# A transformer block and a quantised gated block: the softmax product in runs of four key tiles, q and k stacks in three places, V in two buffers on the chip

## The chip, the core and the metric

One core of a Trainium2 chip runs the whole program in one launch. The metric is the device time in microseconds of one execution; the kernel before took 1111.65 us (median of three runs, 1110.89 to 1113.03). All numbers of a trace come from one profiled execution. In it DVE is VectorE, ACT ScalarE, POOL GpSimd, SP SyncE (it only issues DMAs here), PE TensorE's matmuls and PEld its weight loads; SPq stands for SyncE's queue.

## The reference, cut to what matters

Eight sequences (batches) of 512 tokens with 256 features go through two layers. What the change touches is the attention of the first:

```python
def _ada_rmsnorm(x, t, gamma_w, beta_w):
    return (t @ gamma_w.T)[:, None, :] * _rmsnorm(x) + (t @ beta_w.T)[:, None, :]

def _attention(x, W_q, W_k, W_v, W_o):          # 16 heads of 16 features
    q, k, v = split(x @ W_q.T), split(x @ W_k.T), split(x @ W_v.T)
    attn = softmax(scale * einsum('bnqd,bnkd->bnqk', q, k), axis=-1)
    o = einsum('bnqk,bnkd->bnqd', attn, v)
    return o.transpose(0, 2, 1, 3).reshape(b, l, dm) @ W_o.T

x = x + a_alpha * _attention(_ada_rmsnorm(x, t, ...), W_q, W_k, W_v, W_o)
x = x + f_alpha * _swiglu(_ada_rmsnorm(x, t, ...), gate_w, hidden_w, out_w, out_b)
# then the second layer: rmsnorm, value * gelu(gate), 8-bit rows, ternary down_w, residual
```

## The kernel before

Each engine runs its own program, written out by hand, and they meet at semaphores (`need(engine, name, per, b, k)` waits until `name` has reached `b*per+k`). The attention layer is a software pipeline over the batches: iteration i has 32 slots z, and in each slot every engine does what the timetable (`T_...` constants) puts there for up to three batches, batch i+1 at times 0 to 31, batch i at 32 to 63, batch i-1 from 64. A slot z of the text is such a time modulo 32. The second layer starts in the last slots of iteration 7 and is not touched, but for where its buffers lie.

For a batch the order is: norm, transposed (T_XT1=3), q and k in four pieces (T_QK 7, 8, 10, 11), V in two (T_V 12, 13), then from T_MAX=18 one slot for every two row tiles of maxima, from T_ST=29 one slot m for every two score tiles, the softmax product, and at T_OT=65 the output's turn, its projection (T_OP, slots 4 and 5), the first residual `x1_` (VectorE, one slot later, lines 964 to 969), the second norm (slots 7 to 11), gate and hidden products in slots 14 to 28 and the down products two slots after each.

In TensorE's program a slot is, in this order: `shift_turn` in the four slots in which a group of four heads has all its maxima (times 26, 34, 42, 50, slots 26, 2, 10, 18; L1255), else the first `scores_max` (L1251); two `scores` matmuls (L1265); the weighted product where it is due; the `scores_max` that the turn put off, which waits for VectorE's first two operations on the turned maxima (`shift_c`, L931 and L933); the second `scores_max`; then `turn_o`, projections, q/k/v, gate and down products (L1162), and the turn of a finished group (`turn_group`, L1285). `scores_max` has two banks: matmul n waits for maximum n-2 (`maxima`, L924).

The maxima and scores read `qst` and `kst`, in which q and k of each head stand as six 16-row pieces of bf16 parts (and three rows of negated maxima in `qst`, from `shift`). Those come by way of DRAM: `store_parts` writes q and k parts, `stack` reads them back, 12 DMAs each time. V goes the same way: into `v3` (`v_high`, ScalarE), to `v_d`, and in two halves back to `vst` (`v_load`).

`exp` (ScalarE, L712) writes a pair of heads into one of six places of `p32`, two matmuls' worth per slot. `weighted(b, m)` is one key tile of a group: four heads side by side in the columns of the array, 32 columns each, two instructions each (eight in the trace). It is called twice in every fourth slot, so a block of L1277 has 16 instructions and two key tiles.

SyncE's program is in order, so every DMA waits behind the waits of those before. In an iteration it goes: x2 of two batches ago, al, V's second half, `shift(i, 1)`, `load_xr(i)` (waits until both halves of `x1_` of the batch before are done, L450), `load_xa(i+2)` (L444), parts 0 and 1 of the next batch, `shift(i, 2)`, `stack(nxt, 0)`, parts 2 and 3, `shift(i, 3)`, V's store and first half, `shift(nxt, 0)`, `stack(nxt, 1)`.

Of the kernel before, what the change touches and what calls it, by code (L numbers as in the profile page):

```python
# [16 lines left out]
F32 = mybir.dt.float32  # L17
# [7 lines left out]
P = 128  # L25
# [6 lines left out]
def build(nc, x, cond, w, out):  # L32
# [32 lines left out]
    T_PV = T_ST + 2  # L65
    T_OT = T_PV + STEPS + 2
# [8 lines left out]
    UP_ORDER = (0, 1, 4, 5, 2, 3, 6, 7)  # L75
# [4 lines left out]
    NP_BUF = 6  # L80
    NG = H // GROUP

# [14 lines left out]
    with ExitStack() as ctx:  # L97
# [11 lines left out]
        v_d = nc.dram_tensor("v_d", (B, P, TT, H, VW), F32).ap()  # L109
# [6 lines left out]
        wqkv = [sb(f"wqkv{i}", [P, KD, 3 * D], F32R) for i in range(2)]  # L116
# [33 lines left out]
        v3 = sb("v3", [P, TT, H, VW])  # L150
# [21 lines left out]
        vst_flat = vst[:, :, :, :].rearrange("p t h w -> p (t h w)")  # L172
        n_cw = len(KINDS) * KD * C
        cw = vst_flat[:, 0:n_cw].rearrange("p (n k c) -> p n k c", n=len(KINDS), k=KD)
        raw_o = vst_flat[:, n_cw:n_cw + KD * D].rearrange("p (n i) -> p n i", i=D)
# [6 lines left out]
        wup = [nc.alloc_sbuf_tensor_at(f"wup{n}", [P, KD, 2 * F], F32R, offset=stack_at + n * H * S * 2) for n in range(2)]  # L182
        raw_hp = nc.alloc_sbuf_tensor_at("raw_hp", [P, 2 * KD * S], F32, offset=hp_at)
        v3_flat = v3[:, :, :, :].rearrange("p t h w -> p (t h w)")
        vst_all = vst[:, :, :, :].rearrange("p t h w -> p (t h w)")
        raw_up = [v3_flat.rearrange("p (n i) -> p n i", i=D), raw_hp[:, :].rearrange("p (n i) -> p n i", i=D)]
# [6 lines left out]
        xn_b = tiles_p32[5].rearrange("p (t d) -> p t d", d=D)  # L193
        xr_b = vst_all[:, 0:TT * D].rearrange("p (t d) -> p t d", d=D)
        x1_b = vst_all[:, TT * D:2 * TT * D].rearrange("p (t d) -> p t d", d=D)
        h32_b = qk3[:, :, :, :].rearrange("p a n t -> p (a n t)")[:, 0:2 * KD * S].bitcast(F32).rearrange("p (k t) -> p k t", k=KD)
        qi = [v3_flat.bitcast(BF16)[:, F * n:F * (n + 1)] for n in range(2)]
        qT = [v3_flat.bitcast(BF16)[:, F * (2 + n):F * (3 + n)] for n in range(2)]
# [40 lines left out]
        qk_mm qk_h qk_r qk_m qk_l v_mm v_h parts0_st parts1_st v_st stack0_ld stack1_ld v0_ld v1_ld  # L239
# [8 lines left out]
        s = {n: sem(n) for n in names}  # L248

        def need(eng, name, per, b, k):  # L250
# [95 lines left out]
        def stack_part(eng, st, which, parts, b, tile, h0, h1, name):  # L346

            for g, part in enumerate(parts):
                stack_rows(eng, st, which, g, part, b, tile, h0, h1, name)

        def stack_rows(eng, st, which, g, part, b, tile, h0, h1, name):

            eng.dma_start(st[g * DH:(g + 1) * DH, tile * HT + h0:tile * HT + h1, :],
                          parts_d[bass.ds(b, 1), which, part, tile * P + h0 * DH:tile * P + h1 * DH, :].rearrange("o (h d) t -> d (o h) t", d=DH)).then_inc(s[name], 16)
# [5 lines left out]
        def first_rows(eng, st, which, parts, part):  # L360

            for g, p in enumerate(parts):
                if p == part:
                    stack_rows(eng, st, which, g, part, 0, 0, 0, GROUP, "stack_first")

        @block.sync
        def _(sp):
# [1164 lines left out]
```

## Time and profile before

| | before |
|---|---|
| median of three runs (us) | 1111.65 |
| profiled execution, its own time | 1110.89 |
| its span, first to last instruction | 1109.1 |
| mean granted TensorE clock | 0.980 |
| TensorE busy | 94% |
| VectorE busy | 70% |
| ScalarE busy | 51% |
| GpSimd busy | 31% |
| mean DMA rate | 84 GB/s |

The first attention batch starts its scores at 53 us; from 226 to 720 us six batches follow at 98.8 us each; the second layer alone runs from about 838 us to the end. The clock column of a windows row is the mean granted clock in it, 1.00 being 2.4 GHz and 0.50 1.2 GHz. A matmul's row includes its way through the array, so rows of successive matmuls overlap. "Idle before" is given with what ended it.

### The profile page before, as it was taken

What the parts mean: (1) busy time and instruction counts of PE and PEld (TensorE: products, weight loads), DVE (VectorE), ACT (ScalarE), POOL (GpSimd) and SP (SyncE); (2) the same over time, 40 slices, a digit from 0 to 9 for tenths busy, and PEclk for the clock granted to TensorE, in tenths of its full rate; (3) what the DMA queues carried; (4) which work ended last, traced back from release to release, by engine and by line L of the source; (5) the groups of instructions that cost most, each with busy time, mean ns of one, the idle gap of its engine ahead of it and who ended that gap; (6) DMA issues with size and microseconds to landing.
All of it is one profiled execution on the core that took longest, in us unless ns stands there. A gap on an engine that the chain in (4) does not pass through costs nothing.

```text
span 1109.1 us, 19198 instructions
## 1 busy us (share of the span) xinstructions
PE 1037.1 (94%) x6775; PEld 719.0 (65%) x6775; DVE 774.6 (70%) x1556; ACT 562.6 (51%) x1260; POOL 347.4 (31%) x415
## 2 busy tenths in 40 slices
PE   6789889999999999999999999988989999899997
PEld 5333247755774775577567567744878878788775
DVE  4766686677578757866876696677647787466775
ACT  4355666557556655755665575556552333132221
POOL 2501123323242332424133332201332444243331
PEclk9889999999999999999999999998999999999998
DMA  8554433064234406332531623060311210002111
GB/s 252 150 92 154 76 104 132 15 110 125 87 45 111 148 21 111 101 111 30 121 116 58 111 71 123 12 139 20 97 53 29 59 57 30 29 29 63 58 53 38
DMA packets 89375, 92.71 MB, mean 84 GB/s; under 512 B 11856, under 2 KB 86616, under 8 KB 88256
## 3 DMA queue, kind: packets, MB, share of 16 engines
q1 hardware_dynamic: 87248, 89.59, 31.1%
q10 hardware_dynamic: 2032, 1.90, 0.6%
q8 instruction: 54, 0.88, 0.3%
q14 instruction: 41, 0.34, 0.1%
HBM read 61.68 MB, written 29.78 MB: 82 GB/s over the span
## 4 chain that ended last, share of the span: by engine, by line
PE 77%; DVE 14%; issue 5%; DMA 2%; POOL 1%; ACT 1%; ACTq 0%; POOLq 0%; DVEq 0%
PE gen L1162 30%; PE core L1162 13%; PE pvb L1277 11%; PE core L1251 9%; PE core L1265 8%; DVE negmax L924 7%; PE gen L1488 2%; PE pvb L1480 1%; PE gen L1236 1%; DVE o L948 1%; PE pvb L1285 1%; PE gen L1315 1%; PE core L1255 1%; DVE qs L1112 1%; DMA shift_d<-shift 0%
## 5 line engine op out<-in xcount | busy, mean ns | idle before, releaser
L924 DVE TENSOR_REDUCE negmax<-core 128x1 f32<-128x512 f32 x512 | 337.5, 684 | 169.9 <-PE core L1251 169.0
L712 ACT ACTIVATE p<-core 128x512 f32<-128x512 f32 x512 | 278.5, 597 | 146.1 <-PE core L1265 143.5
L1162 PE MATMUL gen<-hs,wgh 128*128 128x256 f32 x1536 | 220.5, 294 | 9.7 <-DVE a L978 9.7
L1251 PE MATMUL core<-kst,qst 96*128 96x512 bf16 x512 | 193.7, 395 | 33.5 <-DVE negmax L924 27.7
L1162 PEld LDWEIGHTS gen<-hs,wgh 128*128 128x128 f32 x1536 | 196.2, 189 | 28.3 <-DVE a L978 14.8
L1162 PE MATMUL core<-wup,hp 128*128 128x512 f32 x768 | 190.7, 397 | 0.9 <-POOL hp L652 0.9
L603 POOL TENSOR_TENSOR a<-a 128x256 fp32r<-128x256 f32 x128 | 94.7, 740 | 290.3 <-ACT a L730 287.7
L1162 PEld LDWEIGHTS core<-wup,hp 128*128 128x128 f32 x768 | 140.2, 189 | 29.2 <-issue 0.9
L1265 PE MATMUL core<-qst,kst 99*128 99x512 bf16 x512 | 157.2, 387 | 0.1
L1251 PEld LDWEIGHTS core<-kst,qst 96*128 96x128 bf16 x512 | 46.0, 97 | 152.3 <-DVE negmax L924 77.4
L1277 PE MATMUL pvb<-p,vst 128*32 128x512 f32 x1024 | 127.7, 618 | 0.0
L730 ACT CAST a<-a 128x256 fp32r<-128x256 f32 x128 | 52.0, 406 | 126.8 <-DVE a L978 84.4
L1162 PE MATMUL gen<-wout,a 128*128 128x256 f32 x768 | 113.8, 286 | 2.4 <-DVE h L918 1.7
L1162 PEld LDWEIGHTS gen<-wout,a 128*128 128x128 f32 x768 | 100.7, 190 | 4.6 <-DVE h L918 1.9
L1106 DVE TENSOR_TENSOR p<-core,p 128x512 f32<-128x512 f32 x64 | 44.1, 688 | 71.2 <-PE core L1162 50.3
L660 POOL TENSOR_SCALAR v<-p 128x1024 bf16<-128x1024 f32 x32 | 34.5, 1078 | 149.7 <-DVE p L1120 149.7
L725 ACT ACTIVATE th<-gen 128x256 f32<-128x256 f32 x128 | 48.7, 381 | 50.8 <-PE gen L1162 50.1
L1265 PEld LDWEIGHTS core<-qst,kst 99*128 99x128 bf16 x512 | 50.7, 100 | 33.4 <-ACT p L712 6.7
L1277 PEld LDWEIGHTS pvb<-p,vst 128*32 128x32 f32 x1024 | 27.2, 111 | 67.5 <-issue 64.9
L862 ACT ACTIVATE p<-core 128x512 f32<-128x512 f32 x64 | 37.8, 590 | 62.7 <-PE core L1162 62.6
L974 DVE SCALAR_TENSOR_TENSOR ug<-th,gen 128x256 f32<-128x256 f32 x128 | 52.7, 411 | 19.0 <-ACT th L725 18.8
L574 POOL TENSOR_TENSOR hp<-h,hp 128x512 fp32r<-128x512 f32 x15 | 21.5, 1454 | 116.0 <-ACT hp L705 116.0
(158 smaller groups left out, 1234.0 us busy)
## 6 DMA issues: line engine op xcount, KB each, us to landing
parts_d<-qk SPq DMA_DIRECT2D x30, 384.0 KB, 2.7
v_d<-v SPq DMA_DIRECT2D x8, 1024.0 KB, 3.9
vst<-v_d SPq DMA_DIRECT2D x16, 512.0 KB, 5.4
qst<-parts_d SPq DMA_DIRECT2D x96, 64.0 KB, 2.3
qst<-parts_d SPq DMA_DIRECT2D x48, 128.0 KB, 4.5
kst<-parts_d SPq DMA_DIRECT2D x48, 128.0 KB, 7.7
kst<-parts_d SPq DMA_DIRECT2D x91, 64.0 KB, 2.3
xr<-in_x_dram SPq DMA_DIRECT2D x8, 512.0 KB, 4.0
```

Of the source, the lines that this page charges most:

```text
L603: pool.tensor_tensor(a2[1][:, n % 2, :], a32[:, n % 2, :], a2[0][:, n % 2, :].bitcast(F32), ALU.subtract).then_inc(s["a_lo"], 1)
L712: act.activation(p32[:, ring(b, m), k * S:(k + 1) * S], stb[k], ACT.Exp, scale=SCALE).then_inc(s["exp_"], 1)
L725: act.activation(th[:, n % 2, :], gh_bank(b, n)[:, 0:HALF], ACT.Tanh, scale=0.5).then_inc(s["tanh_"], 1)
L730: act.copy(a2[0][:, n % 2, :], a32[:, n % 2, :]).then_inc(s["ah"], 1)
L862: act.activation(ge[:, c, :], smb[c], ACT.Gelu).then_inc(s["gelu"], 1)
L924: dve.tensor_reduce(negmax[:, n // TT, n % TT:n % TT + 1], smb[n % 2], AX_X, ALU.max, negate=True).then_inc(s["smax"], 1)
L974: dve.scalar_tensor_tensor(out=ug[:, n % 2, :], in0=th[:, n % 2, :], scalar=1.0, in1=gh_bank(b, n)[:, 0:HALF], op0=ALU.add, op1=ALU.mult). ...
L1106: dve.tensor_tensor(hb[t % 2][:, c * S:(c + 1) * S], stb[c], ge[:, c, :], ALU.mult).then_inc(s["hmul"], 1)
L1162: last = pe.matmul(out_, l, r, start=start and i == 0, stop=stop and i == len(passes) - 1, **kw)
L1251: pe.matmul(smb[n % 2], qst[0:KROWS, h, q * P:(q + 1) * P], kst[0:KROWS, h, :], start=True, stop=True).then_inc(s["smax_mm"], 1)
L1265: last = pe.matmul(stb[k], kst[0:KROWS + NPART, h, kt * P:(kt + 1) * P], qst[0:KROWS + NPART, h, :], start=True, stop=True)
L1277: last = pe.matmul(pvb[j * VW:(j + 1) * VW, :], vst[:, kt, GROUP * g + j, :], p32[:, ring(b, m - 1 + j // 2), (j % 2) * S:(j % 2 + 1) * S] ...
```

## The change

The two `weighted` calls of every fourth slot become four in every eighth: the product of a group's four key tiles is one run, in times T_PV+7, +15, +23 and +31 with T_PV=30, slots 5, 13, 21, 29. It stands at the end of the softmax part of the slot, after both `scores_max`. `p32` gets eight places. `turn_group`, `o_out` and `heads_out` follow T_PV and come one slot earlier; T_OT and all after it stay. For the room, `qst` and `kst` hold 12 heads instead of 16, in three places of four heads that the groups take in turn (`place`), and each group is loaded by itself: group 3 in its own iteration after `load_xa`, group 0 where tile 0 was, group 1 after `shift(i, 3)`, group 2 where tile 1 was. Each load waits until the group that had the place has all its scores (`place_free`). V no longer goes to DRAM: `v_high` writes into `v0` or `v1` by the batch's parity and the product reads there. In the second layer `wup`, `xn_b` and others lie elsewhere, and the order of eight weight groups differs.

```diff
-    T_PV = T_ST + 2
-    T_OT = T_PV + STEPS + 2
+    T_PV = T_ST + 1
+    T_OT = T_PV + STEPS + 3
...
-    NP_BUF = 6
+    NP_BUF = 2 * KT
     NG = H // GROUP
+    N_PLACES = 3
...
-        qst = sb("qst", [P, H, S], BF16)
-        kst = sb("kst", [P, H, S], BF16)
-        vst = sb("vst", [P, TT, H, VW])
+        qst = sb("qst", [P, N_PLACES * GROUP, S], BF16)
+        kst = sb("kst", [P, N_PLACES * GROUP, S], BF16)
+        v1 = sb("v1", [P, TT, H, VW])
+        vbuf = (v0, v1)
...
+        def place(b, g):
+            return (b * NG + g + 1) % N_PLACES * GROUP
...
-            def stack(b, tile):
+            def place_free(b, g):
+                if g >= N_PLACES:
+                    need_sp("st_mm", 2 * STEPS, b, 4 * GROUP * (g + 1 - N_PLACES))
+                else:
+                    need_sp("st_mm", 2 * STEPS, b - 1, 4 * GROUP * (NG + g + 1 - N_PLACES))
+            def stack(b, g):
                 for n in range(2):
-                    need_sp(f"parts{n}_st", 16 * KD, b, 16 * (tile + 1))
-                pieces = ((0, GROUP, "stack_first"), (GROUP, HT, "stack0_ld")) if tile == 0 else ((0, HT, "stack1_ld"),)
-                for h0, h1, name in pieces:
-                    need_sp("st_mm", 2 * STEPS, b - 1, 4 * (tile * HT + h1))
-                    for st, which, parts in ((qst, 0, Q_PARTS), (kst, 1, K_PARTS)):
-                        stack_part(sp, st, which, parts, b, tile, h0, h1, name)
+                    need_sp(f"parts{n}_st", 16 * KD, b, 16 * (g * GROUP // HT + 1))
+                place_free(b, g)
+                for st, which, parts in ((qst, 0, Q_PARTS), (kst, 1, K_PARTS)):
+                    stack_part(sp, st, which, parts, b, g, STACK[g])
...
                 if here:
-                    v_load(i, 1)
                     shift(i, 1)
                     load_xr(i)
                 if i + 2 < B:
                     load_xa(i + 2)
+                if here:
+                    stack(i, 3)
...
                 if prep:
-                    need_sp("v_h", TT // 2, nxt, TT // 2)
-                    sp.dma_start(v_d[bass.ds(nxt, 1), :, :, :, :].rearrange("o p t h w -> p (o t h w)"), v3[:, :, :, :]).then_inc(s["v_st"], 16)
-                    if i == -1:
-                        sp.wait_ge(s["cw2_t"], 1)
-                        sp.wait_ge(s["wt_t"], 1)
-                    v_load(nxt, 0)
+                    if i != -1:
+                        stack(nxt, 1)
                     shift(nxt, 0)
                 if i == -1:
-                    stack(0, 1)
+                    stack(0, 2)
...
                 if here and prep:
-                    stack(nxt, 1)
+                    stack(nxt, 2)
...
+                    if i == -1 and z == Z_REST + 2:
+                        pool.wait_ge(s["cw2_t"], 1)
+                        pool.wait_ge(s["wt_t"], 1)
+                        pool.memset(v1[:, :, :, DH:VW], 1.0).then_inc(s["v1_ones"], 1)
...
             def v_high(b, j):
                 need(act, "v_mm", TT // 2, b, j + 1)
-                need(act, "v_st", 16, b, 0)
-                act.copy(v3[:, 2 * j:2 * j + 2, :, 0:DH], gen[V_BANK[j]][:, :].rearrange("p (t h d) -> p t h d", t=2, h=H)).then_inc(s["v_h"], 1)
+                need(act, "pv_mm", NG * KT, b - 1, 0)
+                if (b, j) == (1, 0):
+                    act.wait_ge(s["v1_ones"], 1)
+                act.copy(vbuf[b % 2][:, 2 * j:2 * j + 2, :, 0:DH], gen[V_BANK[j]][:, :].rearrange("p (t h d) -> p t h d", t=2, h=H)).then_inc(s["v_h"], 1)
...
             def weighted(b, m):
                 g, kt = m // (2 * KT), m % (2 * KT) // 2
-                if kt == 0 and g % 2 == 0:
-                    need(pe, f"v{g // 2}_ld", 16, b, 16)
+                if kt == 0 and g == 0:
+                    need(pe, "v_h", TT // 2, b, TT // 2)
...
-                    for b, m in stream(z, T_PV):
-                        if m % 4 == 3:
-                            weighted(b, m - 2)
-                            weighted(b, m)
                     for b, g in turned:
                         need(pe, "shift_c", 4 * NG, b, 4 * g + 2)
                         for b2, m in stream(z, T_MAX):
                             scores_max(b2, 2 * m)
                     for b, m in stream(z, T_MAX):
                         scores_max(b, 2 * m + 1)
+                    for b, m in stream(z, T_PV):
+                        if m % (2 * KT) == 2 * KT - 1:
+                            for kt in range(KT):
+                                weighted(b, m - 2 * (KT - 1 - kt))
```

## Rows read from the trace of the kernel before

**Rows 1.** the page's chain that ended last; the windows view of one steady period
```profile
PE 77%; DVE 14%; issue 5%; DMA 2%; POOL 1%; ACT 1%; ACTq 0%; POOLq 0%; DVEq 0%
...
325.47:424.23 98.76, 95.25 (x663) 64.55 (x662) 71.32 (x140) 60.53 (x134) 32.68 (x36) 1.00 0.36 91
```

**Rows 2.** timeline of TensorE, batch 4: start, length, line, count, idle before and releaser
```profile
424.22 0.39 PE L1251 MATMUL core<-kst,qst 96*128 96x512 bf16 x1
...
426.05 0.60 PE L1265 MATMUL core<-qst,kst 99*128 99x512 bf16 x2
426.57 1.92 PE L1277 MATMUL pvb<-p,vst 128*32 128x512 f32 x16
428.43 0.39 PE L1251 MATMUL core<-kst,qst 96*128 96x512 bf16 x1
...
433.02 0.39 PE L1251 MATMUL core<-kst,qst 96*128 96x512 bf16 x1 [1.25 <-DVE negmax L924]
...
440.90 0.39 PE L1251 MATMUL core<-kst,qst 96*128 96x512 bf16 x1
...
458.47 0.60 PE L1251 MATMUL core<-kst,qst 96*128 96x512 bf16 x2
...
462.58 0.39 PE L1251 MATMUL core<-kst,qst 96*128 96x512 bf16 x1
```

**Rows 3.** timeline of VectorE in the same batch
```profile
431.66 0.25 DVE L944 RECIPROCAL orec<-pvb 128x16 f32<-128x16 f32 x1
...
432.28 2.51 DVE L924 TENSOR_REDUCE negmax<-core 128x1 f32<-128x512 f32 x4
...
438.97 1.28 DVE L958 TENSOR_TENSOR hs<-gen,hs 128x512 fp32r<-128x512 f32 x2
...
449.81 0.69 DVE L969 TENSOR_TENSOR x<-ug,xr 128x512 f32<-128x512 f32 x1
```

**Rows 4.** timeline of TensorE's weight loads inside one block
```profile
427.03 0.13 PEld L1277 LDWEIGHTS pvb<-p,vst 128*32 128x32 f32 x4 [0.30 <-issue]
427.46 0.13 PEld L1277 LDWEIGHTS pvb<-p,vst 128*32 128x32 f32 x4 [0.30 <-issue]
```

**Rows 5.** timelines of TensorE and VectorE at the turn of slot 26
```profile
413.13 0.27 PE L1255 MATMUL core<-ident,negmax 128*16 128x128 f32 x1
413.24 0.60 PE L1265 MATMUL core<-qst,kst 99*128 99x512 bf16 x2
...
413.75 0.28 DVE L933 TENSOR_TENSOR shift<-core,shift 16x128 f32<-16x128 f32 x1
```

**Rows 6.** SyncE: timeline of its issues; waits of SyncE, of TensorE (total, times, longest)
```profile
450.53 0.40 SPq L450 DMA_DIRECT2D xr<-in_x_dram  x1
451.02 0.45 SPq L444 DMA_DIRECT2D xa<-in_x_dram  x1
...
472.34 2.77 SPq L353 DMA_DIRECT2D kst<-parts_d  x6
...
SPq L450 <- DVE x L969: 66.6, 7, 10.2
...
PE core L1251 <- DMA kst<-parts_d: 0.8, 1, 0.8
```

**Rows 7.** line 353 between 462 and 475: time from issue to landing
```profile
DMA to landing us min/median/max: 2.1/2.3/3.5
```

**Rows 8.** windows view: last columns clock, share of the DMA engines, GB/s
```profile
426.10:428.10 2.00, 2.00 (x19) 0.47 (x17) 1.22 (x3) 1.40 (x3) 0.73 (x1) 1.00 1.15 140
452.50:456.30 3.80, 3.51 (x20) 2.03 (x19) 3.80 (x9) 3.80 (x9) 1.07 (x2) 1.00 0.79 256
470.50:472.50 2.00, 2.00 (x16) 1.57 (x15) 1.05 (x3) 0.82 (x3) 0.00 (x0) 1.00 0.48 136
```

**Rows 9.** windows view: a thin stretch of batch 0 and what followed it
```profile
98.80:102.60 3.80, 2.30 (x11) 0.68 (x9) 3.40 (x8) 2.17 (x4) 0.00 (x0) 1.00 0.51 139
102.70:106.00 3.30, 3.30 (x17) 0.59 (x16) 0.79 (x4) 1.04 (x2) 0.00 (x0) 0.50 0.72 246
```

More of the change, by code:

```diff
@@ L343, in rows_of, with stack_part, stack_rows @@
             return t[bass.ds(b, 1), :, :].rearrange("o (t p) d -> p (o t) d", p=P)
[L346 to L354, printed above, removed]
+        def stack_part(eng, st, which, parts, b, g, name):
+            for n, part in enumerate(parts):
+                stack_rows(eng, st, which, n, part, b, g, name)
+        def stack_rows(eng, st, which, n, part, b, g, name):
+            h0, r0 = place(b, g), g * GROUP * DH
+            eng.dma_start(st[n * DH:(n + 1) * DH, h0:h0 + GROUP, :],
+                          parts_d[bass.ds(b, 1), which, part, r0:r0 + GROUP * DH, :].rearrange("o (h d) t -> d (o h) t", d=DH)).then_inc(s[name], 16)
         def first_part(eng, which, part, name):
@@ L363, in first_rows @@
                 if p == part:
-                    stack_rows(eng, st, which, g, part, 0, 0, 0, GROUP, "stack_first")
+                    stack_rows(eng, st, which, g, part, 0, 0, "stack_first")
         @block.sync
@@ L413, in first_stack @@
                 first_rows(sp, kst, 1, K_PARTS, 2)
[L414 removed]
+                stack_part(sp, qst, 0, Q_PARTS, 0, 1, "stack1_ld")
                 for name in ("first_kh", "first_km"):
                     sp.wait_ge(s[name], 16)
[L417 to L424 removed]
+                stack_part(sp, kst, 1, K_PARTS, 0, 1, "stack1_ld")
             def shift(b, g):
@@ L431, in shift @@
                 need_sp("shift_st", 16 * (H // GROUP), b, 16 * (g + 1))
-                need_sp("st_mm", 2 * STEPS, b - 1, 4 * GROUP * (g + 1))
-                sp.dma_start(qst[KROWS:KROWS + NPART, g * GROUP:(g + 1) * GROUP, :],
+                place_free(b, g)
+                sp.dma_start(qst[KROWS:KROWS + NPART, place(b, g):place(b, g) + GROUP, :],
                              shift_d[bass.ds(b, 1), :, n0:n1, :].rearrange("o n (h j) t -> (o n) h (j t)", h=GROUP)).then_inc(s["shift_ld"], 16)
@@ L558, in _ @@
             pool.memset(half_pow[:, :], -0.5).then_inc(s["consts_set"], 1)
[L559 removed]
+            pool.memset(v0[:, :, :, DH:VW], 1.0).then_inc(s["consts_set"], 1)
             pool.wait_ge(s["consts_set"], 3)
@@ L844, in first_half @@
                     if b == 0 and t == 0:
-                        last = max(m for m in range(STEPS) if ring(B - 1, m) == NP_BUF - 1)
-                        act.wait_ge(s["pv_mm"], NG * KT * (B - 1) + (last | 3) // 2 + 1)
+                        act.wait_ge(s["st_mm"], 2 * STEPS * B)
                     need(act, f"x2_ld{t}", 16, b, 16)
@@ L1242, in scores_max @@
             def scores_max(b, n):
-                for first, name in ((0, "stack_first"), (TT * GROUP, "stack0_ld"), (TT * HT, "stack1_ld")):
+                for first, name in ((TT * GROUP * g, STACK[g]) for g in range(NG)):
                     if n == first:
@@ L1262, in scores @@
                 for k in range(2):
-                    h = GROUP * g + 2 * pair + k
+                    h = place(b, g) + 2 * pair + k
                     need(pe, "exp_", 2 * STEPS, b, 2 * m + k - 1)
@@ L1276, in weighted @@
                 for j in range(GROUP):
-                    last = pe.matmul(pvb[j * VW:(j + 1) * VW, :], vst[:, kt, GROUP * g + j, :],
+                    last = pe.matmul(pvb[j * VW:(j + 1) * VW, :], vbuf[b % 2][:, kt, GROUP * g + j, :],
                                      p32[:, ring(b, m - 1 + j // 2), (j % 2) * S:(j % 2 + 1) * S], start=(kt == 0), stop=(kt == KT - 1))
```

50 lines of the change are left out of this document (22 added, 28 removed).

## The prediction, made before the changed kernel was run

> **What bounds the kernel now.** I read the page's engine shares and clock first (the table above), then the chain, then one period of the pipeline. The chain that ended last is 77% TensorE and 14% VectorE [rows 1]. One batch sequence takes 98.76 us in the steady part, TensorE busy 95.25 us of it [rows 1]. That figure hides something: one matmul's row is 0.39 us long, yet two in a row are 0.60 [rows 2], so each takes 0.22 us of TensorE and the rest of its row is its way through. I therefore count starts, not busy time. In that measure a slot (two matmuls of L1251 for the maxima, two of L1265 for the scores) takes 0.88 us, the softmax product (L1277) comes in every fourth slot, and in slots 14 to 29 gate and down products fill TensorE completely. In slots 31 to 9 VectorE is the slower engine: before 433.02 TensorE waits 1.25 us for a maximum [rows 2], while VectorE makes four maxima in 2.51 us without a pause [rows 3]. So the kernel alternates between a stretch bound by TensorE and a stretch in which the two take turns, and what an edit is worth depends on which it lands in.
>
> **The merged products.** Before, a block is four groups of four matmuls (two key tiles, two passes each). The weight loads of successive groups start 0.43 us apart (427.03, 427.46) [rows 4]. Four groups are 1.72 us, but the scores end at 426.05+0.22+0.22=426.49, the block starts at 426.57 and the next matmul at 428.43 [rows 2]: it takes 1.94 to 1.95 us. So entering and leaving cost 0.23 us per block. The change makes 32 blocks of eight groups (3.44+0.23=3.67 us) out of 64: it saves 32×0.23=7.4 us, 0.92 per batch. This lies on TensorE and counts in full.
>
> **What the old places covered.** Blocks stood in slots 2, 6, 10, 14, 18, 22, 26, 30; now they stand in 5, 13, 21, 29. The turns of the maxima (L1255) are in slots 2, 10, 18, 26, each of which had a block, and none has one now. After a turn at 413.13 the scores end at 413.24+0.44=413.68; VectorE's second shift operation ends at 413.75+0.28=414.03, and only then may the next L1251 go [rows 5]. The block, which stood there, hid that wait. Without it TensorE waits about 0.40 us. Slots 18 and 26 are in the full stretch: 0.80 us per batch on the path, against 0.46 saved by their two merges.
>
> Slots 29 to 3, with times from the first L1251 of slot 29 (424.22). After: slot 29 is 0.88+3.67+0.72=5.3; slot 30 with down and the group's turn 2.0, to 7.3. Then VectorE sets the pace, at 0.60 a maximum, 0.62 for the heads' output, 0.60 for the scaling, 1.2 for the four shift operations, 1.2 for both residues of o (each the distance between two starts: 432.28-431.66, and (2.51-0.69)/3 or 1.28-0.68 for rows of several [rows 3]): from 7.45 the heads' output, slot 31's maxima and the scaling to 9.9, slot 0's to 11.1, slot 1's until 12.3; the turn starts at 12.4, the shift operations end at 13.9, maxima and residues at 16.35. The next slot's L1251 needs the last maximum before that plus a residue's time: slot 4 starts at 17.1. Before it was 440.90-424.22=16.7 [rows 2]. The blocks that left slots 30 and 2 were partly cover for VectorE, and the time they gave back is gone: +0.4.
>
> **The stack of group 3.** Before, all sixteen heads had their own place, and q and k of the last eight were loaded in the batch sequence before. With three places group 3 must wait for group 0's scores (slot 4), and in SyncE's program it stands behind load_xr, which waits for the first residual (x1_), and behind load_xa. L450 follows the VectorE row of L969 that ends at 450.50, and L444 comes 0.49 us later [rows 3, 6]; SyncE waits 66.6 us for that residual in all [rows 6]. The residual after: slot 4 takes 2.25 (17.1 to 19.4), slot 5 with block and projection 0.88+3.67+1.42, to 25.3; two maxima and two operations of 0.6 and 0.7 end it at 28.4. Then 1.0 us for the issues of xr and xa, eleven spacings of 0.47 between twelve pieces (six take 2.77 us [rows 6]), and 2.3 us for the last to land [rows 7]: at best 28.4+1.0+5.2+2.3=36.9. xr and xa are in front, though; most of their 1 MB moves from 452.5 to 456.3, 5.8 us after the residual, at 256 GB/s [rows 8]. Behind them 0.77 MB of pieces at that rate take 3.0 us and 0.4 for the completion: 37.6. At the 140 GB/s which larger pieces showed between 426 and 428 [rows 8] it would be 28.4+5.8+5.5=39.7. I take 37.6, since the small pieces moved 136 GB/s at a share of only 0.48, the large ones 140 at 1.15 [rows 8]. The Trainium skill ("DMA: Bandwidth & Descriptors", "Anatomy of one DMA") gives, for transfers that GpSimd issues, a fixed 2.0 us plus the bytes at 436 GB/s, 2.15 us for 64 KB. By that estimate the best case would be 36.75 rather than 36.9; the row's 2.3 us is used.
>
> When does TensorE want it? Slot 6 runs 25.3 to 26.6. VectorE ends the residual at 28.4, and then owes the heads' output and slot 7's maxima: slot 8 begins at 29.7, slot 9 at 31.95, the turn of slot 10 at 33.9, its first L1251 at 35.0, which is the first to read group 3. (Before: 458.47-424.22=34.25, with three blocks in it [rows 2].) So the load is late by 2.6 us, bounds 1.9 and 4.7. Behind the waiting L1251 stand the q and k projections of slots 10 and 11. From that L1251 to slot 12 are 462.58-458.47=4.1 us [rows 2]: slot 12 starts at 41.7, before at 38.4. That is +3.3, and with 0.35 for slots 12 to 28 **+3.7 us per batch** (bounds 3.0 and 5.8).
>
> **Everything else.** ACT's first exponential of a group now waits for the first key tile of the block, some 1.4 us; tanh, h_high and the casts queue behind it. The closest is h_high in slot 5, then GpSimd's remainders (2×1.3 us), wanted in slot 7 1.3 us later than I find them done: nothing, or 1 us per batch if that margin is wrong. V: eight stores and sixteen loads go from SyncE's queue; no TensorE or VectorE wait names them, only SyncE's own [rows 6], so nothing gained. The copy of V now waits for the product two batches back, long done. The memset of the second V's ones runs while GpSimd is idle; behind it stand small operations of the next preparation, no price, at most its own microsecond or so. The other stack loads (groups 0, 1, 2 in slots 13, 21, 29) have five slots each of 2 to 6 us against 5.5 us of issue and 2.3 of landing: covered; if slot 29's were late by its whole landing it would cost 2.3 per batch. The tail's new buffers and order touch no row on its path.
>
> **Sum.** Batches 1 to 5: 5×3.7=18.5. Batch 6 has no xa in front (0.5 less): 3.2. Batch 7 has no xa either and no maxima after slot 17, so its late turns cost nothing while the merges save 0.46: 3.3-0.5-0.46=2.3. Batch 0 has no residual to wait for, and no gates: of eight slots two had a block, 0.88+1.95 and that with the turn's 0.11, 5.8 together. Now one has 0.88+3.67 and one the turn, its wait and two maxima, about 1.7: 6.25, or +0.45, four times 1.8. Together 25.8 us, the 7.4 saved already taken off.
>
> **The clock.** Between 98.8 and 102.6 TensorE started only 11 matmuls, and from 102.7 to 106.0 the granted clock was 0.50 (1.2 instead of 2.4 GHz) [rows 9]. In the steady period it stayed 1.00 [rows 1], though slots 31 to 1 are thin there too. After the change slots 31 to 3 are thin for 10 us, and the wait in slot 10 is idle time. A fall costs half of its 3.3 us, about 1.6, if full work follows. I count one fall in every second of seven batches: +5 us (bounds 0 and 11, one in each). By the Trainium skill ("TensorE: Matmul & The Clock Gate", "Why this matters for your kernels") an idle gap between bursts of matmuls puts TensorE back to half rate. That speaks against this change; by it every batch would have its fall, and the sum would be 6 us higher.
>
> The profiled execution took 1110.89 us around a span of 1109.1; the median of three is 0.76 above it. So 1110.89+25.8+5+0.8=1142.5, and I say **1142**.
>
> **Rivals.** (1) *No stack wait*: the load is in time, because the residual comes earlier or the pieces overlap. Then the turns and VectorE's stretches remain: in slots 29 to 9 about +1 net of merges, slots 12 to 28 +0.35, so 1.4 a batch, 10 in all: 1121 (1116 to 1128). For it: a single wait of TensorE for a stack, 0.8 us, is in the trace now [rows 6]. Against it: that stack is loaded with nothing but its slot in the way. (2) *The merges win*: the waits after turns and in slots 31 to 9 are absorbed, since VectorE gets to work ahead during a block. Price 7.4 saved: 1104. It decides if the uncovered wait is under 0.23×32/28=0.26 us; the row says 0.40, and two banks for the maxima let VectorE get only two ahead. (3) *It costs more*: pieces at 140 GB/s (+2.1 a batch) and a clock fall in every batch: 1142+15=1157, up to 1162. (4) *It doesn't do what it says*: the eight groups are torn apart by a late exponential. Its last one is issued a slot before, so no; it would give back the 7.4: 1149.
>
> **Chances.** Forecast (1128 to 1148) 0.48, (3) and (4) 0.18, (1) 0.20, (2) 0.10, no change 0.04. A measurement of this kernel tells 0.2%, some 2.2 us, from nothing. Range: 1118 to 1158, which leaves out (2), no change and the far ends of (1) and (3). Faster 0.10, same 0.04, slower 0.86.
>
> **What would show it.** Blocks of L1277 of 32 rows lasting about 3.65 us; a wait of 0.4 us before L1251 after each L1255; a wait of L1251 for the DMA of kst or qst once per batch of 2 to 3 us, in slot 10; a period of about 102.5 to 103; clock 0.96 to 0.98. Wrong, if that DMA wait is missing (rival 1), or if slots 31 to 3 are shorter than 1.7 us each.

## The result: 3.8% slower, and where the time went

The changed kernel takes **1153.27 us** (median of four runs, 1150.21 to 1156.36) against 1111.27 for the kernel before (four runs, 1108.71 to 1113.03). The ratio is 1.038, 95% interval 1.0349 to 1.0412. The direction was forecast and the time lies in the range of 1118 to 1158, but 11 us above the 1142. The profiled execution of the changed kernel took 1156.36 us around a span of 1154.6.

| | before | after |
|---|---|---|
| median (us) | 1111.27 | 1153.27 |
| span of the profiled execution | 1109.1 | 1154.6 |
| mean granted TensorE clock | 0.980 | 0.959 |
| TensorE / VectorE busy | 94% / 70% | 91% / 67% |
| mean DMA rate | 84 GB/s | 66 GB/s |

The timeline of TensorE shows where each batch's scores start. By those starts (span against span, 45.5 us in all) the loss is distributed so: batch 0 takes 67.7 us instead of 73.9 (-6.2); batch 1 106.4 instead of 99.35 (+7.0); batches 2 to 6 105.2 to 106.1 instead of 98.8 to 99.1 (together +34.3); batch 7 100.35 instead of 94.42 (+5.9); from its last scores to the second layer's first unit 14.2 instead of 11.87 (+2.3); the rest +2.1. Batches 2 to 6 are the steady part, five batches and not six from 226 to 720 us before.

The page of the changed kernel: the clock by slices, then the chain that ended last. VectorE has gone from 14 to 16% of the chain and the engine "issue" from 5 to 6% [rows 1].

```profile
PEclk9799889998999999999989999987998999999998
...
PE 74%; DVE 16%; issue 6%; POOL 1%; DMA 1%; ACT 1%; ACTq 0%; POOLq 0%; DVEq 0%
```

One steady period of it in the windows view (width, busy and count of TensorE, its weight loads, VectorE, ScalarE, GpSimd; clock, share of the DMA engines, GB/s):

```profile
439.06:544.29 105.23, 96.95 (x663) 65.62 (x661) 70.55 (x140) 60.60 (x134) 32.27 (x36) 0.98 0.23 66
```

It has the same 663 rows of matmuls as a period before [rows 1], so nothing was added to TensorE's work. The 6.5 us more went to idle time and to a lower clock. The waits of TensorE (total, times, longest) say at what:

```profile
PE core L1259 <- DVE negmax L932: 29.0, 53, 2.0
PE core L1259 <- issue: 25.1, 7, 4.7
...
PE core L1259 <- DVE shift L941: 6.6, 24, 0.7
```

The second line is the load of group 3. The view names "issue" since it saw no releaser, but it comes seven times, once in each of batches 1 to 7 and always in slot 10. The third is the uncovered turn: 24 waits, where before there was one of 0.7 us. Batch 4 on TensorE's timeline (start, length, ..., idle time before it and its releaser):

```profile
439.06 0.39 PE L1259 MATMUL core<-kst,qst 96*128 96x512 bf16 x1
...
440.02 3.64 PE L1285 MATMUL pvb<-p,v 128*32 128x512 f32 x32
...
452.61 0.60 PE L1259 MATMUL core<-kst,qst 96*128 96x512 bf16 x2 [0.25 <-DVE shift L941]
...
456.18 0.39 PE L1259 MATMUL core<-kst,qst 96*128 96x512 bf16 x1
...
473.14 0.28 PE L1263 MATMUL core<-ident,negmax 128*16 128x128 f32 x1
473.25 0.60 PE L1273 MATMUL core<-qst,kst 99*128 99x512 bf16 x2
477.60 0.59 PE L1259 MATMUL core<-kst,qst 96*128 96x512 bf16 x2 [3.75 <-issue]
477.84 2.22 PE L1170 MATMUL gen<-hp,wqkv 128*128 128x512 f32 x6
```

The block is whole, 32 rows in 3.64 us (so are 30 of the kernel's 32 blocks). After the scores at 473.25 TensorE stands for 3.75 us. The six projection matmuls behind the wait take 2.22 us; with the wait short (the next experiment) they take 1.73. What SyncE issued meanwhile (same batch), and how long those twelve pieces took to land:

```profile
467.66 0.39 SPq L455 DMA_DIRECT2D xr<-in_x_dram  x1
468.15 0.45 SPq L449 DMA_DIRECT2D xa<-in_x_dram  x1
468.72 2.78 SPq L361 DMA_DIRECT2D qst<-parts_d  x6
471.54 2.77 SPq L361 DMA_DIRECT2D kst<-parts_d  x6
...
DMA to landing us min/median/max: 3.6/4.5/5.3
```

The last piece is issued near 473.9 and TensorE goes on at 477.60. Before, the same kind of piece landed in 2.3 us [rows 7]. The windows view shows why (last columns: clock, share, GB/s), and last, what the clock did behind the wait:

```profile
469.60:471.60 2.00, 2.00 (x10) 1.33 (x10) 2.00 (x5) 2.00 (x5) 1.10 (x2) 1.00 0.99 328
471.60:473.60 2.00, 1.97 (x14) 1.24 (x12) 2.00 (x6) 2.00 (x5) 0.00 (x0) 1.00 1.15 282
473.60:475.60 2.00, 0.25 (x2) 0.00 (x0) 1.60 (x5) 1.66 (x4) 1.41 (x2) 1.00 1.15 200
475.60:477.60 2.00, 0.01 (x1) 0.04 (x2) 0.00 (x0) 0.00 (x0) 0.89 (x1) 1.00 1.07 271
...
478.90:482.30 3.40, 3.40 (x9) 1.77 (x9) 2.90 (x5) 1.91 (x4) 0.00 (x0) 0.50 0.01 5
```

The DMA engines are full from 469.6 until the stack has landed, and in this batch, 1.3 us after TensorE starts again, the granted clock is 0.50 (1.2 GHz) for 3.4 us. Such a stretch, called a fall below, begins in or just behind the wait of slot 10 in each of batches 1 to 6 (from 158.0, 263.8, 369.7, 478.9, 581.3 and 687.1; five of them are 6.8 us long), and none in the steady period before [rows 1].

### The profile page after: what moved, and what is told of

The parts are those of the page before. It is cut to its first block, busy times and chain, and to the rows that moved or that the text cites. A ratio compares the mean times of both kernels' runs of the same rounds, so it can differ in the third digit from the quotient of the medians.

```text
span 1154.6 us, 19269 instructions
## 1 busy us (share of the span) xinstructions
PE 1055.1 (91%) x6775; PEld 731.1 (63%) x6775; DVE 771.0 (67%) x1556; ACT 562.8 (49%) x1260; POOL 343.8 (30%) x416
## 4 chain that ended last, share of the span: by engine, by line
PE 74%; DVE 16%; issue 6%; POOL 1%; DMA 1%; ACT 1%; ACTq 0%; POOLq 0%; DVEq 0%
PE gen L1170 30%; PE core L1170 12%; PE pvb L1285 10%; PE core L1259 8%; DVE negmax L932 7%; PE core L1273 7%; PE gen L1498 2%; PE pvb L1490 1%; PE gen L1244 1%; PE pvb L1293 1%; DVE shift L941 1%; DVE shift L939 1%; DVE shift L943 1%; DVE o L956 1%; DMA parts_d<-qk 1%
## 5 line engine op out<-in xcount | busy, mean ns | idle before, releaser
L1259 PE MATMUL core<-kst,qst 96*128 96x512 bf16 x512 | 202.4, 409 | 62.2 <-DVE negmax L932 29.0
L1273 PE MATMUL core<-qst,kst 99*128 99x512 bf16 x512 | 163.1, 398 | 0.3 <-ACT p L719 0.2
L1259 PEld LDWEIGHTS core<-kst,qst 96*128 96x128 bf16 x512 | 47.9, 99 | 156.6 <-DVE negmax L932 74.8
L1285 PE MATMUL pvb<-p,v 128*32 128x512 f32 x1024 | 118.8, 605 | 0.0
L1285 PEld LDWEIGHTS pvb<-p,v 128*32 128x32 f32 x1024 | 30.3, 111 | 73.6 <-issue 73.2
L1170 PE MATMUL gen<-hp,wqkv 128*128 128x512 f32 x192 | 64.0, 475 | 0.0
```

What stands on the lines that cost most here:

```text
L1170: last = pe.matmul(out_, l, r, start=start and i == 0, stop=stop and i == len(passes) - 1, **kw)
L1259: pe.matmul(smb[n % 2], qst[0:KROWS, h, q * P:(q + 1) * P], kst[0:KROWS, h, :], start=True, stop=True).then_inc(s["smax_mm"], 1)
L1273: last = pe.matmul(stb[k], kst[0:KROWS + NPART, h, kt * P:(kt + 1) * P], qst[0:KROWS + NPART, h, :], start=True, stop=True)
L1285: last = pe.matmul(pvb[j * VW:(j + 1) * VW, :], vbuf[b % 2][:, kt, GROUP * g + j, :], p32[:, ring(b, m - 1 + j // 2), (j % 2) * S:(j % 2 + ...
```

## Experiments

All are edits of the changed kernel unless said otherwise. Ratios are against the kernel before, timed on the same chip. "The reordered kernel" is the first of them. Each has one profiled execution, and the number of falls differs between the executions of one kernel, so falls are counted in the profiled one.

**The stack of group 3 loaded ahead of xr and xa.** Its place is free after slot 4, so it need not stand behind load_xr, which waits for the residual.

```diff
                     shift(i, 1)
+                    stack(i, 3)
                     load_xr(i)
                 if i + 2 < B:
                     load_xa(i + 2)
-                if here:
-                    stack(i, 3)
```

> The changed kernel with one edit: group 3's stack is issued before load_xr and load_xa, so that it waits for group 0's scores alone. Theory A (the load behind the residual is the main loss): the idle of 3.75 us before the first L1259 of slot 10 goes, 3.5 us in each of 7 batches, and the clock falls that follow it (1.6 to 2.5 us each) go too; what is left over the kernel before is the uncovered turns and VectorE's stretch, 1.4 us a batch less nothing: 1118 to 1122 us, period 100.1 us. Rival B (the clock falls come from the thin slots 31 to 3, not from the idle wait): the wait goes and the falls stay, one or two per batch: 1128 to 1135 us. Rival C (the stack is late for another reason, such as the rate of its transfers): above 1145 us.

Measured: 1121.29 us (1120.43 to 1125.13), ratio 1.0113 (1.0085 to 1.0142). SyncE issues group 3's pieces from 440.78 now, and nothing is left of the wait in slot 10 but the turn's (batch 4, TensorE's timeline):

```profile
456.83 0.28 PE L1262 MATMUL core<-ident,negmax 128*16 128x128 f32 x1
456.94 0.60 PE L1272 MATMUL core<-qst,kst 99*128 99x512 bf16 x2
457.93 0.60 PE L1258 MATMUL core<-kst,qst 96*128 96x512 bf16 x2 [0.39 <-DVE shift L940]
458.18 1.73 PE L1169 MATMUL gen<-hp,wqkv 128*128 128x512 f32 x6
```

No fall of the clock is left in batches 1 to 6, though slots 31 to 3 are as thin as in the changed kernel. So **the order of one SyncE program cost 32 of the 42 us**, and the falls behind slot 10 came with the wait, not from the thin slots. The settled period is 100.7 to 100.8 us: 1.95 above the kernel before.

**Runs of two key tiles at the old places**, with the loads and V of the changed kernel.

```diff
-    T_PV = T_ST + 1
-    T_OT = T_PV + STEPS + 3
+    T_PV = T_ST + 2
+    T_OT = T_PV + STEPS + 2
...
-                    for b, m in stream(z, T_PV):
-                        if m % (2 * KT) == 2 * KT - 1:
-                            for kt in range(KT):
-                                weighted(b, m - 2 * (KT - 1 - kt))
...
                         scores(b, m)
+                    for b, m in stream(z, T_PV):
+                        if m % 4 == 3:
+                            weighted(b, m - 2)
+                            weighted(b, m)
```

> The changed kernel with the product put back into runs of two key tiles in slots 2, 6, 10 and so on; places, loads and V stay as changed. Theory A: group 3 is still late. The residual ends 26.3 us after slot 29 as before, the load needs 10.0 us from there as in the changed kernel, 36.3, and TensorE wants it at 34.25: 2 us a batch, 14 in all, 1125 us, up to 1135 where the clock falls behind it. Rival D (the loss belongs to the merged runs and their places alone): 1111 us, the kernel before.

Measured: 1123.29 us, ratio 1.0121 (1.0092 to 1.015). Counted from the residual the load takes as long as in the changed kernel (from the issue of xr to the L1259 of slot 10 10.6 us in batch 4, against 9.9; its pieces land in 4.8 us), but the wait is smaller:

```profile
PE core L1259 <- issue: 11.4, 6, 2.6
```

Here the block of 1.92 us stands in slot 10, between the turn and the L1259 that reads the late stack, while in the changed kernel that work stands in slot 5, ahead of the residual on which the load waits. So the blocks that moved away had hidden not only VectorE's shift but would have hidden half of this wait too (12.1 us over seven batches instead of 22.5), and with a shorter idle time only one fall of the clock was seen in batches 1 to 6.

**Both.** The two edits together; what is left of the change is V on the chip, the three places and eight buffers.

> Both edits: runs of two key tiles, and group 3's stack before load_xr. Against the kernel before only the three places, the ring of eight and V on the chip remain. Theory A: these cost nothing once the load is early: 1109 to 1113 us. Rival: keeping V on the chip or the ring of eight has a gain or a price of its own: outside that.

Measured: 1106.23 us (ten runs, 1101.46 to 1111.22; before 1110.55), **ratio 0.9961 (0.9939 to 0.9984)**: faster than both kernels, by a little, and below the 1109 to 1113 that were expected. The steady period is 98.87 to 98.90, that of before. Taking either edit alone leaves 1.1 to 1.2%, both together nothing, neither 3.8%: the parts are not a sum, since the removed cover and the late load meet in slot 10. Alone they cost 10.7 and 12.7 us, together 42. Of the 18.6 us more, 10.4 are the longer waits, and the rest is about what six falls cost instead of one.

**Sixteen heads again**, so that group 3 has a place of its own and is loaded a batch ahead as before. To make room, heads_out's raw output shares the last place of p32 and the second layer's down weights lie in the fourth place of kst.

```diff
-    N_PLACES = 3
+    N_PLACES = 4
...
-                if here:
-                    stack(i, 3)
...
                     stack(nxt, 2)
+                    stack(nxt, 3)
```

> Merged runs of four key tiles and V on the chip, but q and k stacks of all sixteen heads as before, group 3 loaded at the end of an iteration behind group 2 (the room comes from laying the copy of the product and the ternary weights over other buffers). Theory A: the merge alone costs more than it gives, 1.4 us a batch: 1118 to 1122 us, like the first experiment. Rival E (runs of four are a gain, the stacks spoil it): 7 us under the kernel before, 1104 us.

Measured: 1122.28 us, ratio 1.0123 (1.0095 to 1.0151). It agrees with the reordered load within its interval, and no fall is left in batches 1 to 6 either, so it is the late load that cost the 32 us and nothing else about the reordering. Runs of four key tiles are no gain even with every load in time.

**The wait filled with matmuls.** Fifteen matmuls of data that lie ready, whose result nobody reads, are added between the scores of slot 10 and the waiting L1259.

```diff
                     for b, g in turned:
+                        if g == 2 and 1 <= i < B:
+                            need(pe, "o_norm", NG, i, 1)
+                            for _ in range(15):
+                                pe.matmul(pvb[:, :], wo[0][:, 0, 0:P], wo[1][:, :, :].rearrange("p k n -> p (k n)"), start=True, stop=True)
```

> The changed kernel with fifteen matmuls more per batch (of weights, into the idle product bank, 0.236 us each, 3.5 us) between the scores of slot 10 and the maxima that wait for group 3. The load is as late as before. Theory A: TensorE's idle time in slot 10 is what makes the clock fall; with it filled the falls of 1.6 to 2.5 us in each of seven batches go and nothing is added, since the wait was there anyway: 1136 to 1143 us. Rival B (thin slots 31 to 3 make it fall): the falls stay, 1153 us. Rival F (work in the wait isn't free): above 1153 us.

Measured: 1142.36 us (1140.0 to 1147.05), ratio 1.0305 (1.0264 to 1.0347), clock 0.983. A kernel that does more work is 11 us faster. Batch 4 of it:

```profile
466.91 0.60 PE L1273 MATMUL core<-qst,kst 99*128 99x512 bf16 x2
467.16 3.81 PE L1414 MATMUL pvb<-wo 128*128 128x512 f32 x15
471.42 0.59 PE L1259 MATMUL core<-kst,qst 96*128 96x512 bf16 x2 [0.45 <-issue]
471.66 1.75 PE L1170 MATMUL gen<-hp,wqkv 128*128 128x512 f32 x6
```

From the turn's scores to the stack's arrival the same time goes by (4.5 us here, 4.35 in the changed kernel). What changes is the work after it: six projections in 1.75 instead of 2.22 us, and slots 10 to 12 (first L1259 to first L1259) 4.1 instead of 5.7. All six falls of slot 10 are gone: the stretch is 4.06 to 4.11 us in each of batches 1 to 6, where the changed kernel has 5.7 to 7.0. So they are caused by the idle wait and not by the late load as such.

The one fall left in these batches lies elsewhere, in slots 3 and 4 of batch 3, behind a thin stretch (windows view):

```profile
339.50:342.90 3.40, 2.22 (x10) 0.57 (x8) 3.24 (x8) 2.92 (x6) 0.00 (x0) 1.00 0.77 236
342.90:346.30 3.40, 3.40 (x13) 2.40 (x13) 2.10 (x4) 0.98 (x3) 0.00 (x0) 0.50 0.01 4
```

So thin slots can make the clock fall too (rival B), but rarely: once in these six batches, and not in batches 1 to 6 of the reordered kernel, of sixteen heads and of the two kernels below whose turns are covered.

**xa behind the stack.** Only load_xr stands ahead of it.

```diff
+                if here:
+                    stack(i, 3)
                 if i + 2 < B:
                     load_xa(i + 2)
-                if here:
-                    stack(i, 3)
```

> The changed kernel with load_xa issued after group 3's stack instead of before it; load_xr and the residual it waits for are still in front. In batches 1 to 5 the 512 KB of xa leave the way. If the stack is late by the bytes in front of it (the DMA engines' share is 1.0 to 1.15 all that time): 1.9 us less at 270 GB/s, 1143 us (1141 to 1146). If it is late by the issues on SyncE's queue alone: 0.5 us less, 1151 us.

Measured: 1139.06 us (1132.34 to 1144.73), ratio 1.0259 (1.0213 to 1.0305). The pieces' time from issue to landing, in the same batch:

```profile
DMA to landing us min/median/max: 2.4/3.3/4.1
```

So with both loads in front they take 4.5 us, with one 3.3, with none 2.3 (median in the reordered kernel, and [rows 7]). The bytes in front are a price of their own beside their issue: in batches 1 to 5 the L1259 of slot 10 comes 0.8 to 1.8 us earlier, and xa's issue is only 0.5 of it. The saving is larger than expected, since the shorter wait also left three falls in batches 1 to 6, of 3.4 us each, instead of six: behind waits of 3.3, 2.6 and 2.4 us, and none behind 2.1, 2.8 and 2.1.

**The turns covered.** The reordered kernel, and in the two slots of the full stretch that have a turn (18 and 26) the twelve gate and hidden matmuls go ahead of the pair that waits for VectorE's shift.

```diff
+                    gates = [(b, n) for n, t in enumerate(T_GH) for b in at(z, t)]
+                    if turned:
+                        for b, n in gates:
+                            gate_hidden(b, n)
+                        gates = []
                     for b, g in turned:
...
-                    for n, t in enumerate(T_GH):
-                        for b in at(z, t):
-                            gate_hidden(b, n)
+                    for b, n in gates:
+                        gate_hidden(b, n)
```

> The first experiment (1121.3 us) with the twelve gate and hidden matmuls of slots 18 and 26 moved ahead of the maxima that wait for the turned shift. By the prediction's step, an uncovered turn costs 0.40 us; twelve of them lie in the full stretch, so 4.8 us go: 1116.5 us (1115 to 1118), and the waits of L1259 for L941 become a third. Rival: VectorE gets its maxima later and the next slot waits for it instead: 1121 us or more.

Measured: 1129.8 us (1127.36 to 1131.83), ratio 1.0177 (1.0143 to 1.0212). That is **worse** than without, 1121.29, where 1116.5 was expected. Batch 4:

```profile
520.43 0.27 PE L1262 MATMUL core<-ident,negmax 128*16 128x128 f32 x1
520.54 0.60 PE L1272 MATMUL core<-qst,kst 99*128 99x512 bf16 x2
520.79 1.76 PE L1169 MATMUL gen<-hs,wgh 128*128 128x256 f32 x12
522.39 0.61 PE L1258 MATMUL core<-kst,qst 96*128 96x512 bf16 x2
...
524.95 0.39 PE L1258 MATMUL core<-kst,qst 96*128 96x512 bf16 x1 [0.56 <-DVE negmax L931]
...
530.03 0.95 PE L1169 MATMUL gen<-wout,a 128*128 128x256 f32 x6 [0.26 <-POOL a L604]
```

The wait for the shift is gone, and the slot takes 3.25 us (start of its scores to that of the next) instead of 3.61. But the pair of maxima starts 1.85 us after the scores instead of 0.85, behind the gates, VectorE reduces it later, and the next slot's second maximum waits for its bank at 524.95: slot 27 takes 3.75 instead of 3.01. Slot 28 takes 3.50 instead of 3.01, and there the row at 530.03 shows a wait for GpSimd. 0.4 us saved, 1.2 given back. The rival in the expectation (VectorE late) was right for the larger part of that.

**Half a cover.** The reordered kernel again. Of the twelve only the six gate matmuls go ahead; they take 0.9 us, enough for the shift.

```diff
+                    early = [(b, n) for n, t in enumerate(T_GH) for b in at(z, t)] if turned else []
+                    for b, n in early:
+                        need(pe, "a_", NCH, b, n if b == B - 1 else n - 1)
+                        gate_half(b, n, 0)
                     for b, g in turned:
...
-                            gate_hidden(b, n)
+                            if early:
+                                gate_half(b, n, 1).then_inc(s["gh_mm"], 1)
+                            else:
+                                gate_hidden(b, n)
```

> The first experiment (1121.3 us) with only the six gate matmuls (0.71 us) of slots 18 and 26 ahead of the maxima that wait for the turned shift; the six hidden ones stay behind. The shift is ready 0.36 to 0.40 us after the scores, so 0.71 us cover it, and the maxima start 0.3 us later than in the first experiment instead of 1.0. If the price of a turn is 0.40 us and what spoiled the full move was VectorE's late start (0.74 us more in each next slot), then up to 12 times 0.40 go: 1117 us (1115.5 to 1119). If VectorE is late at once, each turn gives back 0.3 or more: 1121 to 1125 us.

Measured: 1125.36 us (six runs, 1120.23 to 1127.86; before on that chip 1113.45), ratio 1.0094 (1.0066 to 1.0122). That is above the 1117 hoped for, but the interval overlaps that of the reordered kernel, so the time decides nothing. The trace is clearer: slots 18 and 26 take 3.22 instead of 3.65 and 3.61, the slots behind them (19 and 27) 0.07 more each, but slot 28 still takes 3.50, where a down product waits for GpSimd:

```profile
529.19 0.95 PE L1169 MATMUL gen<-wout,a 128*128 128x256 f32 x6 [0.26 <-POOL a L604]
```

That gives 0.2 us per batch of the 0.8. Why GpSimd's `a` comes late there when only the gates of slot 26 moved was not followed further.

**V alone on the kernel before**: two buffers on the chip, no stores and loads of V, all else as it was.

```diff
-            def v_load(b, tile):
...
+                act.copy(vbuf[b % 2][:, 2 * j:2 * j + 2, :, 0:DH], gen[V_BANK[j]][:, :].rearrange("p (t h d) -> p t h d", t=2, h=H)).then_inc(s["v_h"], 1)
```

> The kernel before with V kept in two buffers on the chip, nothing else. Theory: V's transfers were on no path; what made the third experiment 4 us faster than the kernel before is that the stack wanted in slot 2 of batch 1 is loaded in smaller pieces, earlier (a wait of 1.74 us and a clock fall there): 1109 to 1112 us. Rival G: V's transfers delayed that stack through SyncE's queue and the DMA engines, so V alone gives it: 1105 to 1107 us.

Measured: 1110.69 us (twelve runs), ratio 0.9995 (0.9974 to 1.0015). V costs and gains nothing, as the prediction had it. So the 0.4% of the best version doesn't come from V alone.

## Why the prediction came out as it did

All times of this section are from the first L1259 of slot 29 of batch 4, 439.06 in the changed kernel.

**Merges.** 3.64 us for 32 rows where 3.67 was forecast, 30 of 32 blocks whole. Right; rival (4) is out.

**Turns.** The working put 0.40 us on each uncovered turn. In the reordered kernel slots 18 and 26 show the idle time of 0.25 us before L1258 and take 0.36 to 0.43 us less once the wait is covered (3.22 to 3.25 instead of 3.65 and 3.61). Right. The idle time alone would not have decided against rival (2), whose limit was 0.26 us; the length of the slots does, and so do the 1121 and 1122 us of the two kernels with every load in time, where it said 1104. That the 0.4 us can be had back was not claimed, and they mostly can't.

**Slots 29 to 3.** Slot 4 begins at 456.18, 17.12 against 17.1. Right.

**The residual.** It decides when the load starts:

```profile
466.94 0.69 DVE L977 TENSOR_TENSOR x<-ug,xr 128x512 f32<-128x512 f32 x1
```

It ends at 28.57, forecast 28.4. The turn of slot 10 stands at 34.08, forecast 33.9. Right.

**The landing** is the first term that was mis-sized. Forecast 37.6 with bounds 36.9 and 39.7; the L1259 goes at 477.60, 38.54, and in batches 2 to 6 at 37.4 to 39.0. The choice of 37.6 took the 256 GB/s of xr and xa and let the pieces follow at that rate, with 0.4 us for completion, a term that no run shows by itself. That left 3.0 us from the last issue (34.6) to the end. The last piece was issued near 473.9 (34.8), where the forecast had it, but TensorE went on only 3.7 us later, though the rate was 200 to 328 GB/s: the engines were at a share of 1.0 to 1.15 to the end, and with fewer bytes in front the pieces land sooner. Over batches 1 to 7 the gap between the last L1259 of slot 9 and the first of slot 10 is 4.6 to 6.7 us, against 2.4 (3.0 in batch 7) in the reordered kernel: 22.5 us of wait in all, where 2.6 times seven is 18.

**Slots 10 to 12** were taken as the 4.1 us of before [rows 2]. In the changed kernel they take 5.7, and 6.3 to 7.0 in the other batches with a fall. All of that is the clock: where no fall follows the late load (the filled wait, and batches 4 to 6 with xa behind) they take 4.1. The reordered kernel, at a clock of 1.00, needs 0.45 us more than before there: its slot 11 takes 2.73 us instead of 2.27, both from scores to scores, and its projections wait 0.19 us there for VectorE's `h` (L917), which is behind. In the changed kernel the 4.1 at full clock says that VectorE has caught up during the wait. With slots 12 to 29, +0.6 instead of 0.35, and +0.9 instead of 0.75 in slots 29 to 9, the reordered kernel's period is 1.95 us over that of before, where the working without the late load implied 1.1 and rival (1) put 1.4.

**The clock** is the term that was furthest off. The mechanism was right: half rate after an idle wait. The count was wrong: one fall in every second batch was forecast, and in the profiled execution each of batches 1 to 6 has one. The price was too low as well: 1.6 us is what the one fall of 3.4 us costs, in batch 4, but five are 6.8 us long and cost 2.2 to 2.9 each. Slots 10 to 12 of batches 1 to 6 together take 13.9 us more than those of the filled wait; forecast were 5, with an upper bound of 11. Between the changed and the reordered kernel, 34.3 us apart by their spans, lie 22.5 of waits and 13.9 of clock, less the 2.7 (six times 0.45) that VectorE catches up, 33.7 in all. The profiled execution was the slowest of four; two of the others had a mean clock of 0.967 instead of 0.959, so they lost less to it. The rule of the Trainium skill that the prediction weighed ("TensorE: Matmul & The Clock Gate", "Why this matters for your kernels"), that an idle gap between bursts of matmuls puts TensorE back to half rate, held in batches 1 to 6 of the changed kernel, and the filled wait agrees with it; among the shorter waits, of up to 2.8 us, of the other kernels some were followed by a fall and some not.

**The signs** that the prediction named: blocks of 3.65 us (3.64), a wait for the shift after each turn (24 of 32; in seven of the others the load comes later), a wait in slot 10 of 2 to 3 us (2.4 to 4.7), a period of 102.5 to 103 (105.2 to 106.1), a clock of 0.96 to 0.98 (0.959). In batches 2 to 6 the period grew by 6.9 us where 3.7 and 0.7 for the clock were forecast: the landing is 0.8 of the difference, the clock 1.6.

**Batch 0** was forecast at +1.8 and is 6.2 shorter. Batch 0 ends, by this count, where batch 1's scores start. The block of group 3 now falls into batch 1 as a whole, where before half of it did: 1.9 us less, which come back in the tail. And batch 0 had three clock falls of 3.4 us before, at 71.9, 102.6 and 119.7; the changed kernel has one, of 6.8 from 117.1, and a clock of 1.00 where the first two were:

```profile
71.90:75.30 3.40, 3.40 (x18) 2.12 (x17) 3.12 (x6) 2.40 (x6) 1.36 (x2) 1.00 0.76 144
```

It isn't shown that the merge did this. The kernel before with V alone changed keeps runs of two, has none of the three falls in its profiled execution, and its batch 0 takes 68.5 us. So the falls of batch 0 come and go, and most of the gain here may be luck.

Batch 1 of the kernel before also held a wait for a stack that the prediction did not look at, and which is gone (it stays with V alone, 2.2 us, and is gone in every other kernel of this document, all of which load each group by itself):

```profile
140.69 0.59 PE L1251 MATMUL core<-kst,qst 96*128 96x512 bf16 x2 [1.74 <-issue]
```

Taken together, batches 0 and 1 of the reordered kernel are 7.3 us shorter than before's.

**Batch 7 and the tail.** Batch 7 was forecast at +2.3, and of the tail's new buffers and order it was said that they "touch no row on its path". Batch 7 is +5.9: its L1259 of slot 10 is 2.2 us later behind slot 9 than in the reordered kernel, and its falls add up to 20.4 us at 0.50, where before they were 10.2. The tail is +2.3 in every kernel with runs of four (14.2 us from the last scores to the second layer's first unit) and 0 in those with runs of two (11.87 to 11.88). The last block can't be cut short:

```profile
858.71 3.64 PE L1285 MATMUL pvb<-p,v 128*32 128x512 f32 x32
```

Everything of the last group waits for all of it, where before half had been done four slots earlier. This is a plain omission: a merged run moves work not only between slots but also to the end, and here it is the 1.9 us that left batch 0. A clock stretch at 0.50 from 868.0 to 874.8 falls on the first units of the second layer and is most of the last 2.1 us.

**The sum.** Of the 45.5 us between the spans 30.8 were forecast (25.8 and 5 for the clock). Batch 0 was set 8 us too high and all else 22.7 too low, which leaves 14.7; the profiled execution lies 3.1 above its median and 0.8 had been added for the kernel before's, so 11 are left between the medians. An error that went the other way, perhaps by the luck of the falls in batch 0, kept the forecast as near as that. **Rival (1)**, no stack wait, is measured by the reordered kernel: 1121.29, forecast 1121, though with 1.95 a batch instead of 1.4, and batch 0 and the tail made up the difference. **Rival (3)**, 1157, was right in one half, the clock fall in each batch, and wrong in the other: the bytes moved at 200 to 328 GB/s and not at 140, and the landing (38.5) was nearer to the forecast's 37.6 than to its 39.7.

What stays open: why the best version is 4 us under the kernel before while its steady period is not shorter. In its profile the gain lies in batches 0 and 1 (0.9 and 1.7) and in batch 7 (1.7), with 1.6 lost before batch 0. The 1.7 of batch 1 is the wait of 1.74 us that is gone, and batch 7 has two falls instead of three; that was read, not tested.

## What to carry to other kernels

When a change moves a block of work, ask of each place it leaves what it was hiding there; here one block hid a 0.4 us turn and would have hidden half of the wait for a late load, and two losses that are 1.1% and 1.2% alone were 3.8% together. An in-order DMA program is a dependency: a load put behind one that waits for a result inherits that wait, and moving one line cost or saved 32 us. When a forecast needs the duration of a stretch behind a new wait, give the clock a term of its own: here the stretch took 4.1 us at full clock, as in the undisturbed trace, and 5.7 to 7.0 behind the wait. And a wait lets a slower engine catch up, so losses that show without it can be gone with it (0.45 us a batch here).

## What the runs showed of the hardware

- An idle wait of 2.6 to 4.7 us on TensorE in an otherwise full stretch went with 3.4 or 6.8 us at 0.50 in each of six batches. The work behind it took 1.6 us more where the stretch was 3.4 us long and 2.2 to 2.9 where it was 6.8. With waits of at most 2.6 us (runs of two) there was one such stretch in six batches, with waits of at most 3.3 (xa behind) three. With fifteen matmuls in the wait there was none behind it in six batches, and the kernel with more work was 11 us faster.
- 64 KB pieces landed in 2.3 us (median) with no larger load ahead, 3.3 behind one load of 512 KB on the same queue and 4.5 behind two. In the last two cases they were issued 0.47 us apart.
- A run of eight groups of four small matmuls takes 3.64 us, one of four groups 1.92: 0.43 us a group, and about 0.2 us for entering and leaving at either length.
